# The opening of a cross-attention kernel, rewritten: loads by chunk, K chunk by chunk, bias fold in two halves

## The reference

```
text_p  = x @ W_text + b_text          # 64 x 256 x 512
audio_p = ctx @ W_audio + b_audio      # 64 x 256 x 512
Q = layer_norm(text_p, g1, beta1);  K = layer_norm(audio_p, g2, beta2);  V = audio_p
alpha = softmax(Q @ K.T / sqrt(512))
h   = (alpha @ V) @ W_out + b_out
out = layer_norm(h + x, g_out, beta_out)
```

## Time and profile before

| what | value |
|---|---|
| median of 3 runs | 1278.85 us (1278.84 to 1280.06) |
| profiled execution, its own time | 1279.1 us |
| its span | 1277.3 us |
| PE busy | 1257.2 us (98%) |
| DVE, ACT, POOL busy | 1078.8, 1054.7, 547.5 us |
| first matmul of the second pair | 55.79 us |

### The profile page before, as it was taken

The page is one execution under the profiler, slowest core; times in us unless marked ns, Lnnn a source line. Parts: engine busy times, 40 slices in busy tenths (PEclk is TensorE's granted clock), DMA queues, the critical chain, the costliest instruction groups (busy, mean ns, idle before and its releaser), DMA issues.

```text
span 1277.3 us, 22559 instructions
## 1 busy us (share of the span) xinstructions
PE 1257.2 (98%) x6648; PEld 1066.4 (83%) x6648; DVE 1078.8 (84%) x1726; ACT 1054.7 (83%) x1789; POOL 547.5 (43%) x545
## 2 busy tenths in 40 slices
PE   6999999999999999999999999999999999999997
PEld 5688888888888888888888888888888888888886
DVE  6678888988888988888888888888889888889888
ACT  6777888888888888888888888888888888888874
POOL 0113554335544335544345544345544355543356
PEclk9999999999999999999999999999999999999999
DMA  7257766768766678766678667688666687667693
GB/s 255 60 162 224 225 191 182 186 202 238 227 169 198 184 216 238 212 178 194 182 227 238 204 170 194 192 234 231 185 187 184 202 243 222 179 189 188 209 233 105
DMA packets 99013, 253.53 MB, mean 198 GB/s; under 512 B 12336, under 2 KB 28208, under 8 KB 90800
## 3 DMA queue, kind: packets, MB, share of 16 engines
q1 hardware_dynamic: 77632, 187.22, 41.8%
q0 software_dynamic: 21360, 66.06, 28.7%
HBM read 137.38 MB, written 49.81 MB: 147 GB/s over the span
## 4 chain that ended last, share of the span: by engine, by line
PE 96%; DVE 2%; ACT 1%; DMA 1%; SPq 1%; issue 0%; ACTq 0%; DVEq 0%
PE wide L326 9%; PE wide L327 9%; PE wide L325 9%; PE score L293 7%; PE score L292 7%; PE score L294 7%; PE wide L294 7%; PE wide L292 7%; PE wide L293 7%; PE wide L382 7%; PE wide L381 7%; PE wide L380 7%; PE turn L334 2%; PE turn L293 1%; PE turn L294 1%; PE turn L292 1%
## 5 line engine op out<-in xcount | busy, mean ns | idle before, releaser
L1123 POOL TENSOR_TENSOR y_rows<-y_rows,betao_row 128x512 f32<-128x512 f32 x120 | 167.0, 1391 | 337.9 <-ACT y_rows L585 226.3
L325 PE MATMUL wide<-xT_hi,wt_hi 128*128 128x512 f32 x512 | 202.5, 395 | 3.4 <-ACT k_cols L545 3.4
L326 PE MATMUL wide<-xT_lo,wt_hi 128*128 128x512 f32 x512 | 202.5, 396 | 0.0
L327 PE MATMUL wide<-xT_hi,wt_lo 128*128 128x512 f32 x512 | 202.5, 396 | 0.0
L292 PE MATMUL wide<-cT_hi,wa_hi 128*128 128x512 f32 x384 | 151.7, 395 | 0.7 <-DVE wa_lo L924 0.7
L544 ACT ACTIVATE squares<-wide,bac_col 128x512 f32<-128x512 f32 x128 | 88.3, 690 | 77.2 <-PE wide L294 77.0
L294 PE MATMUL wide<-cT_hi,wa_lo 128*128 128x512 f32 x384 | 151.6, 395 | 0.0
L293 PE MATMUL wide<-cT_lo,wa_hi 128*128 128x512 f32 x384 | 151.3, 394 | 0.0
L382 PE MATMUL wide<-wao_hi,pcT_lo 128*128 128x512 f32 x372 | 146.7, 394 | 0.0
L380 PE MATMUL wide<-wao_hi,pcT_hi 128*128 128x512 f32 x372 | 146.6, 394 | 0.0
L381 PE MATMUL wide<-wao_lo,pcT_hi 128*128 128x512 f32 x372 | 146.5, 394 | 0.0
(11 more groups left out here) (145 smaller groups left out, 3515.6 us busy)
## 6 DMA issues: line engine op xcount, KB each, us to landing
xT_in<-in_xT SPq DMA_DIRECT2D x32, 1024.0 KB, 9.0
xT_lo<-xT_in POOLq DMA_DIRECT2D x31, 1024.0 KB, 8.9
y_rows<-in_x_rows SPq DMA_DIRECT2D x124, 256.0 KB, 4.0
y_rows<-bao_row POOLq DMA_DIRECT2D x31, 1024.0 KB, 9.4
out<-y_rows SPq DMA_DIRECT2D x124, 256.0 KB, 3.3
cT_in<-in_cT SPq DMA_DIRECT2D x32, 768.0 KB, 8.7
c_kept<-in_c_rows SPq DMA_DIRECT2D x32, 768.0 KB, 7.5
p_out<-probs SPq DMA_DIRECT2D x31, 512.0 KB, 4.6
```

The costliest lines, as they stand in the source:

```text
L325: nc.tensor.matmul(wide[h][:], wt_hi[:, d, cols], xT_hi[:, d, :], start=(d == 0), stop=False)
L326: nc.tensor.matmul(wide[h][:], wt_hi[:, d, cols], xT_lo[:, d, :], start=False, stop=False)
L327: done = nc.tensor.matmul(wide[h][:], wt_lo[:, d, cols], xT_hi[:, d, :], start=False, stop=(d == DT - 1))
L1123: nc.gpsimd.tensor_tensor(rows, rows, betao_row[:], ALU.add).then_inc(y_ready, 1)
```

## The change

Only the first pair's order and what feeds it is changed; steps 1 to 31 keep their orders (they are moved into functions `products`, `casts` and `parts`).

- SP loads W_audio, the first cT, W_text and the first xT in chunks of 128 rows (256 KB), alternately, each with its own semaphore. The six column vectors come packed by the host as one array of 128 x 6 x 4 in one DMA.
- PE transposes W_audio chunk by chunk (four blocks into one bank, `waT_bank`: `score[0]`, `score[1]`, `turn[1]`), so `wide` is free at once. K is made chunk by chunk, four tiles per chunk, over the four `wide` banks (`first_k`).
- Chunk 0's mean is made by DVE, those of chunks 1 and 2 by ACT (an activation with a running sum). W_text's means are made by DVE a chunk at a time.
- Q is made in pieces (`first_q`), tiles 0 and 1 alternating, and half of the bias fold, now in `score[1]`, stands between the first two pieces; the other half stands behind the first weight fold. Q's mean square stands ahead of folds 1 and 2.
- The waits for the folded weights move from the end of the first step to pair 1's K products (`wao_split`), and the wait for the folded bias stands inside the scores.

```diff
-        wa_stage, wt_stage, wo_stage, waT_stage = k_cols, q_cols, y_rows[1], y_rows[0]
...
+        wa_stage, wt_stage, wo_stage = k_cols, q_cols, y_rows[1]
+        waT_stage = y_rows[0]
+        waT_bank = [score[0], score[1], turn[1]]
...
+            wa_of, wt_of = (w.rearrange("(t p) h -> p t h", p=P) for w in (w_audio, w_text))
+            for d in range(CT):
+                sp.dma_start(wa_stage[:, d, :], wa_of[:, d, :]).then_inc(wa_loaded[d], 16)
+                sp.dma_start(cT_in[:, d, :], cT[0, :, d, :]).then_inc(cT0_loaded[d], 16)
+                if d == 0:
+                    sp.dma_start(cols[:], columns).then_inc(columns_loaded, 16)
+            for d in range(DT):
+                sp.dma_start(wt_stage[:, d, :], wt_of[:, d, :]).then_inc(wt_loaded[d], 16)
+                sp.dma_start(xT_in[:, d, :], xT[0, :, d, :]).then_inc(x0_loaded[d], 16)
...
-                if isinstance(i, int) and i == 0:
-                    pe.wait_ge(waT_copied, h + 1)
+                if isinstance(i, int) and i == 1 and h < CT:
+                    pe.wait_ge(wao_split, h + 1)
                 wait(pe, y_summed, T * (i - 2) + h + 1)
...
+            def first_k(d):
+
+                pe.wait_ge(cT_split, d + 1)
+                pe.wait_ge(wa_split, d + 1)
+                for h in range(HT):
+                    cols = slice(h * P, (h + 1) * P)
+                    nc.tensor.matmul(wide[h][:], wa_hi[:, d, cols], cT_hi[:, d, :], start=(d == 0), stop=False)
+                    nc.tensor.matmul(wide[h][:], wa_hi[:, d, cols], cT_lo[:, d, :], start=False, stop=False)
+                    done = nc.tensor.matmul(wide[h][:], wa_lo[:, d, cols], cT_hi[:, d, :], start=False, stop=(d == CT - 1))
+                    if d == CT - 1:
+                        done.then_inc(k_done, 1)
...
+            def first_q(h, d):
+
+                if d == 0:
+                    pe.wait_ge(k_centred, h + 1)
+                if h == 0:
+                    pe.wait_ge(wt_split, d + 1)
+                    pe.wait_ge(x0_split, d + 1)
...
+            def fold_bias(part):
+
+                if part[0] == 0:
+                    pe.wait_ge(waT_copied, CT)
+                    pe.wait_ge(wo_loaded, 16)
+                for h in part:
+                    done = nc.tensor.matmul(score[1][:], ba_col[:, h:h + 1].broadcast_to([P, P]), wo_stage[:, h, :],
...
+            turn_wa(0)
+            turn_wa(1)
+            first_k(0)
+            turn_wa(2)
+            pe.wait_ge(columns_loaded, 16)
+            nc.tensor.matmul(turn[0][:, 0:HT], ones, ba_col[:], start=True, stop=True)
+            nc.tensor.matmul(turn[0][:, HT:2 * HT], ones, bt_col[:], start=True, stop=True).then_inc(b_spread, 1)
+            first_k(1)
+            first_k(2)
...
+            def first_products():
+                first_q(0, 0)
+                fold_bias(range(HT // 2))
+                first_q(1, 0)
+                for d in range(1, DT - 1):
+                    first_q(0, d)
+                    first_q(1, d)
+                for d in range(DT - 1):
+                    first_q(2, d)
+                for h in range(HT - 1):
+                    first_q(h, DT - 1)
+                mean_squares(0, turn[0][:], k_sq_parts, k_var)
+                for d in range(DT):
+                    first_q(3, d)
+                fold_weights(0)
+                fold_bias(range(HT // 2, HT))
+                mean_squares(0, turn[1][:], q_sq_parts, q_var)
+                fold_weights(1)
+                fold_weights(2)
...
+                if first:
+                    pe.wait_ge(bao_made, 1)
                 scores(i, 1, 0)
                 scores(i, 1, 1)
-                if first:
-                    pe.wait_ge(wao_split, CT)
-                    pe.wait_ge(bao_made, 1)
...
+            def wa_mean_of(d):
+
+                act.wait_ge(wa_loaded[d], 16)
+                nc.scalar.activation(squares[:, d, :], wa_stage[:, d, :], ACT.Identity, scale=-1.0 / H,
+                                     accum_out=wa_mean[:, d:d + 1]).then_inc(wa_averaged, 1)
...
+            c0_high(0)
+            wa_high(0)
+            for d in range(1, CT):
+                wa_mean_of(d)
+                c0_high(d)
+                wa_high(d)
+            for d in range(CT):
+                waT_copy(d)
+            x0_high(0)
+            wt_high(0)
...
+            def first_casts():
+                for d in range(1, DT):
+                    x0_high(d)
+                    k_centre(0, d - 1)
+                    wt_high(d)
+                k_centre(0, HT - 1)
+                cT_high(1, 0)
+                cT_high(1, 1)
+                move_half(0, turn[0], k_summed, k_moved)
+                q_centre(0, 0)
+                q_centre(0, 1)
+                rstd_of(0, turn[0], k_var, k_log, k_rstd)
+                q_centre(0, 2)
+                q_centre(0, 3)
+                k_high(0, 0)
+                k_high(0, 1)
+                move_half(0, turn[1], q_summed, q_moved)
+                k_high(0, 2)
+                k_high(0, 3)
+                wao_high(0)
+                rstd_of(0, turn[1], q_var, q_log, q_rstd)
+                q_high(0, 0)
+                wao_high(1)
+                q_high(0, 1)
+                xT_high(1, 0)
+                q_high(0, 2)
+                xT_high(1, 1)
+                q_high(0, 3)
+                xT_high(1, 2)
+                xT_high(1, 3)
+                wao_high(2)
...
-            dve.wait_ge(wa_loaded, 16)
-            weights_means(wa_stage, CT, wa_mean, wa_summed, wa_mean_made)
+                nc.vector.tensor_tensor(bao_row[:], score[1][:], bao_row[:], ALU.add).then_inc(bao_made, 1)
+
             for d in range(CT):
+                if d == 0:
+                    weights_mean(wa_stage, d, wa_mean, wa_loaded, wa_summed, wa_mean_made)
...
+                weights_mean(wt_stage, d, wt_mean, wt_loaded, wt_summed, wt_mean_made)
+                x0_low(d)
+                weights_low(wt_lo, wt_hi, wt_stage, d, wt_mean, wt_hi_made, wt_split)
...
+            def first_parts():
+                pair_squares(0, k_squared, k_paired)
+                add_square(0, k_paired, k_squared, k_added)
+                sum_squares(0, k_squared, k_added, k_summed)
+                halve_sum(0, turn[0], k_moved, k_halved)
+                split_sum(0, q_var, 0, k_halved, k_sq_hi, k_sq_parts)
+                cT_low(1, 0)
+                cT_low(1, 1)
+                for h in range(HT):
+                    k_norm(0, h)
+                add_square(0, q_paired, q_squared, q_added)
+                sum_squares(0, q_squared, q_added, q_summed)
+                k_low(0, 0)
+                halve_sum(0, turn[1], q_moved, q_halved)
+                split_sum(0, k_var, 1, q_halved, q_sq_hi, q_sq_parts)
+                k_low(0, 1)
+                k_low(0, 2)
+                k_low(0, 3)
+                q_split(0)
+                make_bao()
+                for d in range(CT):
+                    wao_low(d)
+                cT_low(1, 2)
+                maxima(0, 0)
+                maxima(0, 1)
+                turn_p(0)
+                invert_sums(0)
```

More of the change, by code:

```diff
@@ L690, in step @@
                     xT_high(i + 1, 3)
+            def step(i, odd, first=False, last=False):
+                late = not isinstance(i, int) or i >= 2
                 if first:
-                    wao_high(2)
+                    first_casts()
+                else:
+                    casts(i, odd, last)
                 if not last:
@@ L1025, in step @@
                 maxima(i, 1)
-                if not first and not last:
+                if not last:
                     y_sum(j, 1 - odd, 3)
@@ L1036, in step @@
                     invert_sums(i)
+            def step(i, odd, first=False, last=False):
+                if first:
+                    first_parts()
+                else:
+                    parts(i, odd, last)
             run_steps(dve, step)
```

251 lines of the change are left out of this document (103 added, 148 removed).

## The result

After takes 1277.38 us (median of 22 runs, 1276.32 to 1278.41), before, measured beside it, 1279.28 (22 runs, 1278.38 to 1281.56). By the medians that is 1.9 us, or 0.15%, less; the ratio of the runs is 0.9982, 95% interval 0.9976 to 0.9987, so the gain is small but clear of the noise. The forecast was 1272.6 with a range of 1270.4 to 1275.8: the sign was right, two thirds of the gain are missing.

The account below looks back on a forecast made before the run. PE's matmul stream was taken as the bound, so only the opening counts: pair 1's K 6.0 us earlier, its Q 6.0 to 6.7, taken as 6.2, making 1278.85 into 1272.6; range 1270.4 to 1275.8.

Parts of the forecast that it names:

- Part 1: Opening loads in chunks: first W_audio chunk usable at 4.2 us (0.8 lag included) instead of 5.59.
- Part 2: K by chunk: starts at 7.05 instead of 10.19, ends at 17.55; clock loss taken as 1.0, bounds 0 and 2.4.
- Part 3: First pair's Q in pieces: idles of 2.2 and 0.9 and the 1.5 at lower clock go; Q ends at 30.75.
- Part 4: Weight folds: new idle of 0.8 at Q's second mean, folds end at 43.6, scores end at 49.75.
- Part 5: After the opening: pair 1's Q stalls 0.8 to 1.4 for x's accumulating DMA, gain 6.0 to 6.7; later pairs 0.
- rival A: Opening clock: comes up later (price 1.4) and drops again at the new idle (1.5); 1275.5 with both, chance 0.15.
- own range: Whole kernel: 1270.7 to 1275.1 us, by first chunk's time, clock loss and late Q split.
- rival B: Pair 1's x: accumulating DMA still lands near 65.7, nothing won, 1278.8; half of it 1275.7; chance 0.06.
- C: Opening loads: chunks' fixed times do not overlap, last x lands at 61, about 1310 us; chance 0.02.
- D: First pair's order: a wait is missed, gain only 2 to 4 us, 1275.5; chance 0.12.
- pair 1's first Q product later than 60: Sign of being wrong at the second pair's Q: its first product starts after 60 us.
- any PE wait in the middle of the run: Sign of being wrong in the loop: PE shows any wait there, where none was expected.

Follow-up runs that it names:

- e3: After with 96 unused bytes ahead of xT_in, which puts its large tiles back at before's addresses; 1273.35 us, ratio 0.9962.
- e8: e3 with pair 1's low part of x made by four DVE subtractions instead of ACT's pass and POOL's accumulating DMA; 1272.02 us.
- e2: After, unchanged, profiled again; 1276.84 us, ratio 0.999 to before.
- e5: After with 96 unused bytes ahead of the weights, so weights and everything behind them move together; 1277.33 us.
- e1: Before, unchanged, profiled again; 1278.0 us, ratio 1.0002.
- e12: Before with only the packed column vectors in one DMA, which lowers its large tiles by 96 bytes; 1279.73 us, ratio 1.0004.
- e4: Before with 32 unused bytes ahead of xT_in, so all tiles behind the columns lie 32 bytes higher; 1284.25 us.
- e11: After with bac_col and btc_col merged into one tile, so all behind lies 32 bytes lower; 1258.19 us.
- e13: After with e11's single tile, e8's x low part, e10's order of Q and K, and three small tiles moved ahead of pcT_hi; 1254.46 us.
- e14: e12 with e11's single tile, so the old opening at distance 0; 1262.06 us.
- e15: e11 with 32 unused bytes ahead of the weights, so weights and large tiles move together; 1258.64 us.
- e16: e13 with Q's and K's split tiles 64 bytes higher, distances unchanged; 1254.5 us.
- e6: After with 32 unused bytes ahead of xT_in, moving only what lies behind the columns; 1268.28 us.
- e9: e8 with 32 unused bytes instead of 96 ahead of xT_in, and 128 more ahead of pcT_hi; 1264.7 us.
- e10: e9 with Q's tiles allocated ahead of K's, 64 bytes between them, and 64 bytes ahead of pcT_hi; 1257.34 us.
- e7: After with 64 unused bytes ahead of xT_in, moving only what lies behind the columns; 1277.79 us.

## Why the prediction was wrong, by its steps

| step | predicted | after |
|---|---|---|
| first transpose (Part 1) | 4.2 | 3.48 |
| first K product (Part 2) | 7.05 | 6.22 |
| K ends | 17.55 | 16.47 |
| Q ends (Part 3) | 30.75 | 30.78 |
| new idle at the second mean (Part 4) | 0.8 | 0.70 |
| scores start | 43.6 | 43.59 |
| pair 1's K starts | 49.75 | 49.84 |
| x's accumulating DMA issued (Part 5) | near 47.3 | 48.20 |
| it lands | 59.0 | 60.8 |
| lead at pair 1's Q | 6.0 to 6.7 | 4.84 |
| pairs 2 to 31 | 0 | -3.0 |
| gain in the span | 6.2 | 1.8 |

**Parts 1 to 4** hold in this execution within 1.1 us, the starts of the scores and of pair 1's K within 0.1 us. The first chunk came 0.7 earlier than the 4.2 taken. The rule of the Trainium skill ("DMA: Bandwidth & Descriptors", "Anatomy of one DMA") had put it at 3.3, nearer to the 3.48 of the trace than my lag of 0.8 did; that section gives it for DMAs that GpSimd issues, and these are SP's, so this is one agreement and no test of it.

PE's slow matmuls lasted to 8.06 (starts 0.43 apart, as in e3 at a granted clock of 0.50; the granted clock of 6 to 8 us reads 1.00 all the same), a loss of 1.0 as taken. But this term varies: in e8, e3 and e2 they last until 9.53, 10.38 and 10.73, and in e5 all 12 of chunk 0 are slow, until 11.51, which is the bound of 2.4 and the first half of rival A. The first Q product starts at 16.47 in after, 18.19 in e2, 18.44 in e5, and the second pair's K at 49.84, 50.70, 50.94: after's profiled execution had the fastest front of these, and the agreement to 0.1 us is partly luck.

On the rule of the Trainium skill that was weighed in Part 2 ("TensorE: Matmul & The Clock Gate", Part 4: transposes don't count as activity) these runs are divided: in before's profiled execution the clock was up with nothing ahead of K but transposes and column products, in after the first five of K's own matmuls are slow (6.22 to 8.37, 2.15 us instead of 1.17), in e1, before again, the first eight (10.50 to 14.00). I had called the trace against the rule; one execution was too little for that.

The 1.1 us won by the end of K was spent again before Q's end (three small losses that Part 3 had at nothing): PE waited 0.48 for W_out ahead of the bias fold and 0.21 ahead of K's mean (27.65), and gave 0.4 where the first Q matmul behind the fold stands 0.63 ahead of the next (19.19, 19.82). That Q's end agrees to 0.03 is therefore luck too. (The sums come out as written, but for the low end of the own range: 1272.6 less 0.75 and 1.0 is 1270.85, not 1270.7.)

**Part 5, first miss: 1.4 us** (6.2 taken, 4.84 there). The step was "the DMA lands at 59.0 and PE arrives at 58.25: a stall of 0.8 to 1.4". ACT's pass ended at 47.56, not at 46.7: its first Q cast started at 39.66, after 1.05 us of waiting for DVE's q_cols, and the last one ended at 44.2 instead of 43.2. POOL's row in after:

```profile
48.20 1.07 POOL L1217 DMA_DIRECT2D xT_lo<-xT_in  x1 [18.73 <-ACT xT_lo L560]
```

and the landing of this tile's transfers in after, over the run, the longest being the first (11.6 in the earlier trace rows):

```profile
DMA to landing us min/median/max: 6.9/8.9/12.6
```

The issue was 0.9 later than 47.3, and the transfer took 12.6 instead of 11.6; PE arrived at 58.40 (60.90 less 2.50), near the 58.25 worked out. In e2 the issue came at 49.05 and the transfer took 11.5: it landed 0.2 earlier than in after. PE arrived 0.86 later and so waited 1.40 instead of 2.50, but the Q product started at 60.66, 0.24 from after's. The landing sets this start, not PE's arrival, in both, and neither reaches the 59.0 of the prediction. This miss is rival B in small: the part of the lead that this chain does not follow is given back.

**Part 5, second miss and the one that decides: 3.0 us.** The step was "Pairs 2 to 31 and the tail keep their orders: 0". The orders are kept, the cost is not: 29 pairs are 0.10 us longer each, because the packed column tile moved their operands. e3 shows it from one side (old places, old pair, 3.5 us back), e12 and e4 from the other (old order, new place, longer pair). Terms: 36 K by 0.9 ns are 0.03, the 30 Q matmuls behind the mean by 0.9 are 0.03, 30 of the output by 1.1 are 0.03, 48 scores by 0.3 are 0.01: 0.10 us. The 18 Q matmuls ahead of the mean of K's squares take 4.26 us in both and add nothing. Had I been right on this step alone, the forecast would have been met within 1.5 us: e3's 4.7 under the before beside it against 6.2. Without the stall too (e8, which does more than the change) 6.75 were won.

**The rivals.** A (clock): neither half in after; the first in e5, as said, and in e3 a second drop, behind the stall and not at 36. B: a part of it, above. C (chunks one after another) is refuted, the three K chunks were in by 10. D came nearest in size (1275.5, a gain of 2 to 4 us, against 1277.38 and 1.9), but by a mechanism that is not the one found: it looked for a missed wait, and the larger loss has none. Of my own signs for being wrong, "pair 1's first Q product later than 60" did come (60.90) and points at the first miss; "any PE wait in the middle of the run" could not have seen the second.

## What to carry to other kernels

A change that adds, merges or resizes a small on-chip tile moves every tile allocated behind it; where TensorE is the bound, compare the distance of starts of the same matmul in an untouched stretch before and after, since neither the busy share, nor the waits, nor the printed duration shows it. Follow one instruction per iteration through both traces: a lead that shrinks steadily is a price per iteration, one that shrinks at one place is a wait. Where a kernel repeats one product thousands of times, try its operands at several distances with one unused tile of 32 bytes: here the best step of this kind (e11, 19.2 us) was worth ten times what the whole change brought (1.9), and four times what the new opening brings at unchanged places (4.7 in e3).

## What the runs showed of the hardware

**The pitch of matmuls depends on the distance between the operands' tiles.** For 128x512 fp32r matmuls with a weight load each, at a granted clock of 1.00, the mean distance of starts in ns by the distance (moving minus stationary tile, modulo 256 bytes in a partition):

| distance | K | output product | kernels |
|---|---|---|---|
| 0 | 227.4 to 228.0 | 226.7 to 227.8 | e11, e13, e14, e15, e16 |
| 32 | 233.3 | | after, e5, e12 |
| 64 | 228.8, 229.0 | 228.9 or 233.3 (means 231.1, 233.0) | e6, e9, e10 |
| 96 | 233.4 | 233.3 | e7, e4 |
| 128 | 232.4 | 232.3 | before, e3, e8 |
| 160 | 234.3 | 234.4 | e4, e7 |
| 192 | | 233.7 | e6 |
| 224 | | 233.4, 233.5 | after, e5, e12 |

Two pairs of kernels with equal distances and different own addresses (after and e5; e11 and e15) agree to 0.4 ns, so it is the distance and not the own address. For K and Q every kernel with one distance had one pitch, to 0.6 ns. For the output product the distance is not the whole rule: at 64 its starts, from the sixth on, are 228.9 ns apart in some pairs of e9 and e10 and 233.3 in the others, in one program. For the scores (128x256) distance 0 gave 119.6 to 119.9 ns, and 64 gave, again from the sixth start on, 113.3 in the pairs of e10 whose output product is at 233.3 and 117.8 in the two where it is at 228.9, as in all of e13 and e16 (behind 226.7 and 227.1). The mechanism behind all this is not shown. Only distances that are multiples of 32 were tried.

**When PE's clock comes up in front varies between executions of one kernel.** Before had its matmuls of 0.63 us between 22.83 and 26.42; in e1, the same kernel, they stand at 11.07 to 13.20 and none at Q, where PE had waited 1.22 instead of 2.01. The second pair's K starts at 55.79 and 55.68 all the same. So the 1.5 us that Part 3 took away as the price of the idle of 2.0 us was there in one execution and not in the other. The length of an idle alone does not tell whether a slow stretch follows: one did behind 1.94 (e12), 2.01 (before) and 2.43 us (e3), none behind 1.22 (e1), 1.40 (e2) and 2.50 (after).

**The same 1 MB accumulating DMA landed after 11.5 (e2) to 12.6 us (after) at this place, 8.9 in the median over the run.** That spread of 1.1 us is as large as the stall that was to be predicted (0.8 to 1.4).
